# The main pass of a four-layer block: indirect writes issued sooner, affines split around their wait, one group of statistics later, two transposes swapped

## The reference, cut to what matters

```python
attn = softmax(x @ window.T / 16) @ window      # attend, attended
x1   = norm(x + attn) * g1 + be1                # stats_1st, affine_1st
gate = sigmoid([x1, mo] @ Wg.T + bg)            # gates, merged, tanh
x2   = norm(x1 + gate*x1 + (1-gate)*mo) * g2 + be2   # stats_2nd, affine_2nd
x3   = norm(x2 + silu(x2 @ W1.T + b1) @ W2.T + b2) * g3 + be3   # stats_3rd, affine_3rd
x    = x + norm(x3)                             # stats_4th, nmean_4th, norm_4th, new_x
# second layer: the row's statistics (stats_5th, root5), its expert and its
# place there (route1, route2), and the row written to that place (scatter)
```

## Time and profile before

| | us |
|---|---|
| time, median of 3 runs | 1881.32 (1877.03 to 1881.6) |
| the profiled execution: its span, first to last instruction | 1884.6 |
| PE busy | 1787.1 (95%) |
| PEld busy | 1576.6 (84%) |
| DVE busy | 1467.6 (78%) |
| ACT busy | 1067.6 (57%) |
| POOL busy | 632.8 (34%) |

### The profile page before, as it was taken

The page is one execution under the profiler, slowest core; times in us unless marked ns, Lnnn a source line. Parts: engine busy times, 40 slices in busy tenths (PEclk is TensorE's granted clock), DMA queues, the critical chain, the costliest instruction groups (busy, mean ns, idle before and its releaser), DMA issues.

```text
span 1884.6 us, 31885 instructions
## 1 busy us (share of the span) xinstructions
PE 1787.1 (95%) x11647; PEld 1576.6 (84%) x11647; DVE 1467.6 (78%) x3884; ACT 1067.6 (57%) x1760; POOL 632.8 (34%) x927
## 2 busy tenths in 40 slices
PE   8999999999999999999989999999998799999996
PEld 7888878888888888887868998898987699999996
DVE  7877578899888989888857888489898566666663
ACT  5656735566655566665636664466563355555552
POOL 3212001224343433333452444234545323333233
PEclk9999999999999999999999999999999799999998
DMA  5445242232222211110133441333522222322210
GB/s 180 163 153 168 79 157 61 78 101 97 91 88 84 84 60 60 60 64 32 47 99 128 134 129 58 94 121 114 168 90 78 90 65 86 96 84 81 71 52 18
DMA packets 132756, 177.23 MB, mean 94 GB/s; under 512 B 11502, under 2 KB 115829, under 8 KB 132472
## 3 DMA queue, kind: packets, MB, share of 16 engines
q1 hardware_dynamic: 121848, 160.13, 26.4%
q0 software_dynamic: 10752, 15.06, 2.3%
HBM read 113.52 MB, written 76.51 MB: 101 GB/s over the span
## 4 chain that ended last, share of the span: by engine, by line
PE 70%; DVE 14%; POOL 6%; issue 5%; ACT 3%; DMA 2%; SPq 0%; another core or an unknown queue 0%; POOLq 0%; DVEq 0%; ACTq 0%
PE ps L390 65%; POOL d_p L2657 4%; PE ps L414 3%; DVE bst L1672 2%; DVE xl L1686 1%; DVE xl L1691 1%; POOL smalls L2653 1%; DVE xl L1946 1%; PE ps L706 1%; DVE x2l L1697 1%; PE ps L475 1%; DVE pay L1997 1%; DVE rO L2224 1%; POOL smalls L2652 1%; DMA qc<-in_Wg1T 0%
## 5 line engine op out<-in xcount | busy, mean ns | idle before, releaser
L390 PE MATMUL ps<-wslotA,fh 128*128 128x256 f32 x1776 | 326.3, 284 | 2.0 <-DVE el L1888 2.0
L390 PEld LDWEIGHTS ps<-wslotA,fh 128*128 128x128 f32 x1776 | 280.4, 191 | 7.7 <-DVE el L1888 2.2
L1888 DVE TENSOR_TENSOR fl<-fF,fh 128x512 fp32r<-128x512 f32 x316 | 212.5, 684 | 85.0 <-ACT fF L1242 83.9
L390 PE MATMUL ps<-wslotA,fl 128*128 128x256 f32 x888 | 251.2, 283 | 0.0
L2652 POOL TENSOR_TENSOR smalls<-smalls,powers 128x4 f32<-128x4 f32 x87 | 29.8, 343 | 595.5 <-DVE smalls L1675 595.3
L2657 POOL DMA_INDIRECT d_p<-pay,sut x128 | 158.1, 1235 | 76.3 <-issue 38.3
L390 PE MATMUL ps<-x2h,wslotA 128*128 128x512 f32 x512 | 177.1, 409 | 0.0
L390 PEld LDWEIGHTS ps<-wslotA,fl 128*128 128x128 f32 x888 | 170.0, 191 | 0.0
L1241 ACT ACTIVATE fh<-ps,b1e 128x512 fp32r<-128x512 f32 x126 | 86.9, 690 | 143.0 <-PE ps L390 121.6
L390 PE MATMUL ps<-wslotB,fh 128*128 128x256 f32 x752 | 137.0, 283 | 0.4 <-DVE fl L1888 0.4
L390 PE MATMUL ps<-eh,wslotB 128*128 128x512 f32 x384 | 125.3, 393 | 2.4 <-DVE el L2069 2.4
(11 more groups left out here) (397 smaller groups left out, 4997.3 us busy)
## 6 DMA issues: line engine op xcount, KB each, us to landing
stage<-in_w SPq DMA_DIRECT2D x16, 1024.0 KB
d_p<-blank SPq DMA_DIRECT2D x24, 528.0 KB, 5.3
pay<-d_p SPq DMA_DIRECT2D x24, 528.0 KB
d_x<-df SPq DMA_DIRECT2D x16, 516.0 KB, 3.5
xA<-d_x SPq DMA_DIRECT2D x16, 516.0 KB
xa<-in_x SPq DMA_DIRECT2D x16, 512.0 KB, 4.9
d_h<-hh SPq DMA_DIRECT2D x16, 512.0 KB, 5.4
d_h<-hl SPq DMA_DIRECT2D x16, 512.0 KB, 2.7
```

Source lines behind the costliest of these rows:

```text
L390: return pe.matmul(o, a, b, start=start, stop=stop, skip_group_check=True)
L1888: ve.tensor_tensor(dl[:, half(k)], df_[:, half(k)], f32(dh[:, half(k)]), ALU.subtract).then_inc(S["low"], 1)
```

## The change

Four edits of order, all in the main pass. No arithmetic is added or taken away.

1. **GpSimd**: `scatter(0, s-2)` moves from behind the factors of the fourth and second norm to ahead of them, directly behind the factor of the third norm.
2. **VectorE**: an affine's first half, which needs only the mean, is placed ahead of the wait for the factor. It waits for the statistics of its own engine instead, and the wait for the factor stands between the halves. All three affines of all groups have this.
3. **VectorE**: `stats_5th(0, s-1)` moves from ahead of `affine_1st(s+2)` to behind `lows(x2l, s+1)`.
4. **TensorE**: the transposes `t_t(0, s-1)` go ahead of `x_t(s+3)`; in the ring TT and XT change places.

```diff
@@ tensor_program, loop of the main pass
                     ff_in(s, 3, 1)
+                if s - 1 in GROUPS:
+                    t_t(0, s - 1)
                 if s + 3 in GROUPS:
                     x_t(s + 3)
-                if s - 1 in GROUPS:
-                    t_t(0, s - 1)
                 if s in GROUPS:
                     w2(s, 2)
@@ vector_program
-            def affine(x, t, gain, shift, ready):
+            def affine(x, t, gain, shift, known, ready):
                 m, r = mv_of(t)[:, :, 0], t[:, 12:16]
-                ve.wait_ge(*ready)
+                ve.wait_ge(*known)
                 marks = [mark(ve.scalar_tensor_tensor(x[:, i, :], x[:, i, :], m[:, i:i + 1], gain, ALU.subtract, ALU.mult))
                          for i in range(4)]
+                ve.wait_ge(*ready)
                 out_ = []
...
-                affine(xw(xl[g % 4]), sm(0, g), g1_r, be1_r, (S["rs1"], g + 1))[3].then_inc(S["x1"], 1)
+                affine(xw(xl[g % 4]), sm(0, g), g1_r, be1_r, (S["var1"], g + 1), (S["rs1"], g + 1))[3].then_inc(S["x1"], 1)
...
@@ vector_program, loop of the main pass
                     low(s, 3, 1)
-                if s - 1 in GROUPS:
-                    stats_5th(0, s - 1)
                 if s + 2 in GROUPS:
                     affine_1st(s + 2)
                 if s + 1 in GROUPS:
                     lows(x2l, x2h, ring.of("X2T", s + 1), S["x2h"], s + 1)
+                if s - 1 in GROUPS:
+                    stats_5th(0, s - 1)
                 if s - 2 in GROUPS:
                     route2(0, s - 2)
@@ pool_program, loop of the main pass
                     root(sm(2, s), (S["var3"], s + 1), S["rs3"])
+                if s - 2 in GROUPS:
+                    scatter(0, s - 2)
+                if s in GROUPS:
                     root(sm(3, s), (S["var4"], s + 1), S["rs4"])
                 if s + 2 in GROUPS:
                     root(sm(1, s + 2), (S["var2"], s + 2 + 1), S["rs2"], eps4c)
-                if s - 2 in GROUPS:
-                    scatter(0, s - 2)
                 if s + 3 in GROUPS:
                     root(sm(0, s + 3), (S["var1"], s + 3 + 1), S["rs1"])
```

More of the change, by code:

```diff
@@ L1951, in affine_2nd @@
             def affine_2nd(g):
-                affine(xw(xl[g % 4]), sm(1, g), g2_r, be2_r, (S["rs2"], g + 1))[3].then_inc(S["x2"], 1)
+                affine(xw(xl[g % 4]), sm(1, g), g2_r, be2_r, (S["var2"], g + 1), (S["rs2"], g + 1))[3].then_inc(S["x2"], 1)
             def biased(g):
@@ L1967, in affine_3rd @@
             def affine_3rd(g):
-                affine(xw(xl[g % 4]), sm(2, g), g3_r, be3_r, (S["rs3"], g + 1))[3].then_inc(S["x3"], 1)
+                affine(xw(xl[g % 4]), sm(2, g), g3_r, be3_r, (S["var3"], g + 1), (S["rs3"], g + 1))[3].then_inc(S["x3"], 1)
             def stats_4th(g):
```

## The result

The changed kernel takes 1852.19 us (median of 4 runs, 1850.88 to 1854.24); the kernel before, run beside it, 1879.17 us (4 runs, 1876.08 to 1881.6). The ratio is 0.9851, 95% interval 0.9838 to 0.9864: faster by 27.0 us. Forecast was 1849, own range 1843 to 1856. All times are in us.

What follows compares the result with a forecast made beforehand. TensorE, plus its wait chain through VectorE's affine and GpSimd's late factor, bounds the kernel. Stalls 17.6 and 3.6, falls 10.3 and 1.6, together 33.1, less 1, give gain 32: 1881.3 - 32 = 1849 us, own range 1843 to 1856.

Steps and rivals of the forecast that it cites:

- The stalls: TensorE's waits for lows(x2l), 17.0 us in nine pieces plus 0.61 in step 3, and 3.6 at step 13, all go.
- The allowance of 1 us for residual waits: Taken off the gain, 0.1 us a step, for TensorE waits that show up once the large one is gone.
- The falls: Clock falls behind stalls go: 2.06 us in each of steps 5, 7, 9, 11, 13, so 10.3.
- Phases on VectorE: In the loop, lows(x2l) 1.9 us ahead of TensorE, PF freed 0.75 ahead, later work in the same phase as before.
- rs4: Fourth norm's factor, now behind the scatter, 1.7 us early to 0.9 late; writes 4.8 to 7.4; cost nothing.
- slack of 3.1: In the loop, up to 3.1 us of VectorE lateness from a late rs4 never reaches TensorE.
- rival C: Scatter before rs4 drawn out; gain of 3 us a step eaten from 6.1 us late; 1890 us, 3%.
- The split: Affines' first halves ahead of the factor wait: nothing left to hide in the loop; nothing taken, at most 1.67 us.
- The swap: Transposes in the other order on TensorE: nothing, within 0.1 us a step either way.
- Behind the loop: Epilogue and everything after it shifted whole, since its chain starts with TensorE's last w2.
- the slow stretch behind the last stall: Clock fall after the stall ending step 13 goes: (1 - 0.92) x 20.4 = 1.6 us.
- rival B: A second chain, stats_5th before route2 or late rs4, costs TensorE 0.8 us in 10 steps; gain 20, 1861 us, 10%.

Runs made afterwards that it cites:

- e1_scatter: Kernel before with one edit alone: the four indirect writes directly behind the third norm's factor; 1860.4 against 1887.77 us, ratio 0.9852.
- e4_fill: Kernel before, with TensorE's scores computed twice from step 4 on, 2.4 us more work a step laid into the stall; 1887.12 us, ratio 0.9993.
- e7_double: Changed kernel with each step's four indirect writes issued a second time, into a buffer nothing reads; 1912.35 us, ratio 1.0182 to the kernel before.
- e3_both: Kernel before with the scatter edit and the later stats_5th, without split affines and swapped transposes; 1859.48 us, ratio 0.9853.
- the second time: Changed kernel itself, unedited, run and profiled again beside later runs; 1859.81 us, ratio 0.9837 to the kernel before.
- e8_tail: Changed kernel with stats_3rd(13) moved behind lows(x1l, 15), in step 13 alone; 1849.93 us, ratio 0.9843 to the kernel before.
- e8_again: Changed kernel with stats_3rd(13) behind lows(x1l, 15), run again beside the changed kernel; 1859.62 us, ratio 0.9834 to the kernel before.
- e9_split: Kernel before with one edit alone: the affines' first halves ahead of the wait for the factor; 1859.84 against 1878.5 us, ratio 0.9899.
- e5_no_scatter: Changed kernel with the indirect writes put back behind rs2's factor and ahead of rs1's; 1877.64 us, ratio 0.9991 to the kernel before.

## Why the prediction was right

*The stalls.* Forecast for steps 4 to 13: 17.0 + 3.6 + 10.3 - 1 = 29.9. Measured: 443.47 - 413.51 = 29.96. Step 3, forecast 0.61, gave 0.76 (42.62 to 41.86); step 2 nothing. This was the bulk of the sum, and it came out by its own mechanism: the scatter alone (`e1_scatter`) takes ten of eleven stalls away.

*The allowance of 1 us for residual waits.* There are no waits. Steps 4 to 13 of before, as one window, were

```profile
436.16:879.63 443.47, 422.88 (x2782) 0.98 0.22 74
```

The idle time fell by 20.6 (20.59 to 0.02), all of the stalls, and the busy time by 9.4 (422.88 to 413.49), where I had 10.3 for the falls. The allowance was right by its size and not by its reason, which was luck. I took the fall as the difference of two neighbouring steps, 45.50 - 43.44 = 2.06, but an odd step has 0.4 more work than an even one. Busy time against the same step of the changed kernel fell from 43.62 to 41.84 where there was a fall (1.78, four times; step 13, 1.5) and from 41.58 to 41.44 where there was none: the falls were 8.6 for 10.3, and 0.7 came from the other steps.

*The falls.* Steps of 41.4 to 41.9, all at 1.00, as forecast in their mechanism; their size was 0.3 to 0.5 too large each. That they follow stalls was an inference from the earlier trace rows; `e4_fill` shows it.

*Phases on VectorE.* Forecast: `lows(x2l)` 1.9 ahead of TensorE. It starts at 471.53 and is over at 472.73; `x1_t` starts at 474.53, 1.8 later. Forecast: PF freed 0.75 ahead. Its reader ends at 474.67, and TensorE starts there at 475.35: 0.7. From `x1_t` to `stats_3rd` are 3.13, forecast 3.36.

*rs4.* Forecast: 1.7 early to 0.9 late, writes of 4.8 to 7.4. Measured: the writes take 5.35 to 7.7, rs4 is in time in nine of eleven steps and 1.2 late in two, which doesn't reach TensorE. The price of nothing was right. My slack of 3.1 is only half confirmed: in `e7_double` TensorE's waits behind the late rs4 begin about there, but the steps lose all but 1.5 of what VectorE waits. A lateness of 1.2 costs nothing; how far it is from the edge no run shows. The turning point of rival C, 6.1 of lateness, was too high: 4.79 cost 3.2 a step in `e7_double`, doubled writes included.

*The split.* "Nothing" is right beside the scatter edit (`e3_both`) and wrong as a statement on the split: alone it gives 1.0%. *The swap*: nothing, as forecast, with the split in `e3_both`.

*Behind the loop*, the term that failed. I wrote that "the epilogue and everything behind it is shifted whole", and took 1.6 for the slow stretch behind the last stall. The slow stretch did go (clock 1.00 from 846.6 to 851.0; 0.61 before from 879.6 to 884.0), but the epilogue grew by 2.2, or 1.1 the second time. TensorE now comes to the last `x1_t` without a stall and goes straight to the gates of group 15, whose `x1l` VectorE has only after PF's work, `stats_5th` and `stats_3rd`:

```profile
853.22 0.39 PE L390 MATMUL ps<-x2h,wslotA 128*128 128x512 f32 x1
855.06 0.70 PE L390 MATMUL ps<-small,hh 128*128 128x512 f32 x2 [1.45 <-DVE x1l L1698]
```

That is of rival B's kind, once and not ten times. In place of +1.6 stands -1.1 to -2.2, so 2.7 to 3.8 of the 5 us between forecast gain and measured gain.

Most of the 2.2 isn't the change's. The epilogue ends with eight indirect writes, on which the first experts' rows wait. They begin 83.8 after the last `x1_t` before, 84.4 in the changed kernel and 84.7 the second time; and the eight issues take 10.0 before, 11.5 in the changed kernel and 10.0 the second time. The first and the last of the changed kernel's:

```profile
931.05 1.07 POOL L2658 DMA_INDIRECT d_p<-pay,sut  x1 [0.17 <-POOL s5t L2696]
...
941.13 1.44 POOL L2658 DMA_INDIRECT d_p<-pay,sut  x1 [0.30 <-issue]
```

Over the twelve profiled executions other than `e7_double`'s they take either 10.0 or 11.5, also in two executions of one kernel, and these 1.5 are the larger part of the 2.2. What is left to the change is 0.6 to 0.9. In `e8_tail` and `e8_again`, where both the slow stretch and the wait are gone, the writes begin at 83.5 and 83.9. By these two the slow stretch was worth nothing at the end of the epilogue: the term should have been 0 and not 1.6. The starts of like kernels differ by more than that, though (83.7 to 85.4 in the six with a stall at the last `x1_t`, 83.5 to 84.7 in the others), so that 0.6 to 0.9 isn't clear of the scatter either. What fills the rest of the 5 stays open; it lies outside the loop's forecast, which held, or in the one profile of the loop before.

*The level.* 1849 missed 1852.19 by 3.2, and luck made that small. The forecast is a median less a gain, 1881.3 - 32; the span and its 3.3 drop out of it. The gain was 5 too large, and the median of three runs that it started from 2.1 too high: the fourth run brought it to 1879.17. From there the same sum gives 1847.

## What to carry to other kernels

Before an edit is priced, ask which wait it cures: two edits that cure one wait (writes out of the way, or the affine's first half into the wait) don't add, and one that only reorders work behind a wait costs time until the wait is gone. Fill a stall with useless work to learn whether a clock fall belongs to it, and compare a step with the same step of a kernel without stalls, not with its neighbour. Price lateness by the length of the steps and not by the waits alone: the waits that are listed may be half of it. Where a steady loop is mended, look at its last pass, where the order behind it differs, and at what the stage behind it ends on.

## What the runs showed of the chip

Stalls and the clock: stalls of 1.87, one a step, cost a second time, by a fall to 0.50 for some 4 us behind every second one, 1.78 each; stalls of 0.5 a step had none (`e9_split`); two of 0.6 and 0.8 a step, 1.1 us of work apart, had them in four steps (`e5_no_scatter`); with the time filled there were none (`e4_fill`). Behind a single last stall there was a fall at 3.6 and at 2.3 and none at 1.6 (`e4_fill`, `e9_split`, `e1_scatter`). Steps 4 to 12 took 399.3 with stalls of 1.87 and 380.4 with stalls of 0.5: the last 1.4 us of such a stall were worth 2.1 a step.

An indirect write's issue on GpSimd takes 0.97 by itself and up to 3.38 beside VectorE. The one at 482.96 ended at 486.32, 0.92 after VectorE's unbroken run of operations with two on-chip inputs had ended at 485.4:

```profile
483.21 1.67 DVE L1692 SCALAR_TENSOR_TENSOR xl<-xl,smalls,rows 128x256 f32<-128x256 f32 x4
484.80 0.68 DVE L1889 TENSOR_TENSOR fl<-fF,fh 128x512 fp32r<-128x512 f32 x1
485.40 1.40 DVE L1672 BATCH_NORM_STATS2 bst<-xl 128x6 f32<-128x256 f32 x4
```

Before, the issue of 3.28 ended 0.93 after such a run. The Trainium skill (SBUF — State Buffer, section Who interferes with whom) infers that `tensor_tensor`, with both inputs in SBUF, leaves descriptor generation alone. The coincidence of the ends, in both kernels, suggests that some part of an issue is held up all the same. It isn't shown: the issue ahead of it, 1.50 at 481.15, began and ended inside the same run of VectorE, and no run here took VectorE's operations away.

Executions repeat unevenly: the loop takes 496.8 to 496.9 in six profiled executions of four kernels, while experts and linear attention take 527.3 to 536.4, and the median of the kernel before is 1878.5 in one set of runs and 1889.7 in the next on the same chip. A gain of a few us can be read in the loop, and not in the total.
